# Attention in a fused two-layer kernel: the product of the probabilities with v in two double pieces instead of four single ones

## What is computed

```python
h = gelu(x @ Wi[e] + bi[e]);  x = layernorm(h @ Wo[e] + bo[e] + x) * gamma[e] + beta[e]
x = layernorm(x) * (1 + scale) + shift
q, k, v = x @ Wq + bq, x @ Wk + bk, x @ Wv + bv          # 16 heads of 16 features
scores = q @ k.T / 4 + attention_bias;  scores[masked keys] = -inf
ctx = softmax(scores) @ v                                 # per head: 512 x 512 times 512 x 16
x = x + ctx @ Wo + bo
out = x + gelu2((layernorm(x) * g2 + beta2) @ W1 + b1) @ W2 + b2
```

## Time and profile before

| | us |
|---|---|
| median of 3 runs | 1060.66 (1059.63 to 1061.37) |
| the profiled execution | 1060.56 |
| its span, first to last instruction | 1058.7 |
| attention, 340 to 820 us of the span: PE busy | 464.5 of 480 |
| ACT / DVE / POOL busy in the same stretch | 456.2 / 426.9 / 392.5 |

### The profile page before, as it was taken

The page is one execution under the profiler, slowest core; times in us unless marked ns, Lnnn a source line. Parts: engine busy times, 40 slices in busy tenths (PEclk is TensorE's granted clock), DMA queues, the critical chain, the costliest instruction groups (busy, mean ns, idle before and its releaser), DMA issues.

```text
span 1058.7 us, 19427 instructions
## 1 busy us (share of the span) xinstructions
PE 1006.1 (95%) x6870; PEld 758.3 (72%) x6936; DVE 840.7 (79%) x1966; ACT 790.2 (75%) x1291; POOL 634.2 (60%) x333
## 2 busy tenths in 40 slices
PE   5999999999799999999999999999999799999998
PEld 4789988888565655656666665666666589999997
DVE  6599999998868988989889898998988555555553
ACT  6755577555599899999999999999999344444443
POOL 3565766664246877798787997878877332222110
PEclk9999999999899999999999999999999999999999
DMA  8746788759799999998999989999895131111001
GB/s 234 263 146 222 247 295 301 276 180 378 304 330 398 409 373 358 352 340 322 367 355 340 357 322 362 345 347 343 313 338 199 40 120 60 60 61 40 21 20 40
DMA packets 103249, 269.44 MB, mean 254 GB/s; under 512 B 7522, under 2 KB 63586, under 8 KB 86642
## 3 DMA queue, kind: packets, MB, share of 16 engines
q1 hardware_dynamic: 103154, 268.21, 70.5%
HBM read 217.57 MB, written 50.61 MB: 253 GB/s over the span
## 4 chain that ended last, share of the span: by engine, by line
PE 49%; DVE 12%; DMA 12%; POOL 10%; ACT 8%; issue 7%; SPq 2%; DVEq 0%; ACTq 0%; POOLq 0%
PE psH L540 11%; DMA t_bt<-in_fside_Bx16xSxS 10%; PE psO L540 10%; PE psT L650 9%; POOL t_bt L1423 8%; PE psQ L540 5%; PE psV L663 5%; PE psS L639 4%; ACT t_bt L894 3%; DVE t_x L1026 2%; SPq L255 2%; PE psA L540 2%; ACT t_pt L780 2%; DVE t_bt L1215 2%; PE psX L692 1%
## 5 line engine op out<-in xcount | busy, mean ns | idle before, releaser
L1423 POOL TENSOR_TENSOR t_bt<-t_bt,t_mb 128x1024 f32<-128x1024 f32 x182 | 384.6, 2147 | 89.0 <-DMA t_bt<-in_fside_Bx16xSxS 88.8
L1215 DVE CUSTOM_DVE_ANT_0 t_bt<-psS,t_bt 128x512 f32<-128x512 f32 x512 | 338.2, 684 | 61.1 <-PE psS L639 39.6
L894 ACT ACTIVATE t_bt<-t_bt,t_nm 128x512 f32<-128x512 f32 x512 | 356.6, 732 | 20.4 <-DVE t_nm L1215 20.3
L650 PE MATMUL psT<-t_idf,t_bt 128*128 128x128 f32 x2048 | 308.6, 274 | 5.2 <-issue 2.5
L650 PEld LDWEIGHTS psT<-t_idf,t_bt 128*128 128x128 f32 x2048 | 252.9, 141 | 66.0 <-ACT t_bt L894 12.7
L780 ACT ACTIVATE t_pt<-psT 128x512 f32<-128x512 f32 x317 | 191.2, 603 | 18.9 <-PE psT L650 18.2
L639 PE MATMUL psS<-t_ks,t_qs 128*128 128x512 bf16 x482 | 183.9, 382 | 8.0 <-DVE t_nm L1215 3.7
L1225 DVE COPY t_pt<-psT 128x512 f32<-128x512 f32 x195 | 133.8, 686 | 1.7 <-PE psT L650 1.7
L663 PE MATMUL psV<-t_pt,t_vs 128*17 128x512 f32 x1024 | 134.2, 598 | 0.0
L639 PEld LDWEIGHTS psS<-t_ks,t_qs 128*128 128x128 bf16 x512 | 50.0, 98 | 83.0 <-DVE t_nm L1215 62.8
L1357 POOL TENSOR_SCALAR t_crs<-t_cmv 128x4 f32<-128x4 f32 x8 | 4.2, 519 | 134.8 <-DVE t_cmv L1018 134.8
(11 more groups left out here) (171 smaller groups left out, 2045.1 us busy)
## 6 DMA issues: line engine op xcount, KB each, us to landing
t_bt<-in_fside_Bx16xSxS SPq DMA_DIRECT2D x128, 1024.0 KB, 7.4
sc_qk<-t_parts SPq DMA_DIRECT2D x32, 768.0 KB, 6.6
t_qs<-sc_qk SPq DMA_DIRECT2D x16, 1024.0 KB, 9.8
t_ks<-sc_qk SPq DMA_DIRECT2D x16, 1024.0 KB, 12.2
t_wo_f<-in_L_cond_Wo SPq DMA_DIRECT2D x8, 1024.0 KB, 7.5
sc_qk<-t_parts SPq DMA_DIRECT2D x16, 512.0 KB, 7.4
t_wi_f<-in_L_cond_Wi SPq DMA_DIRECT2D x7, 1024.0 KB, 5.3
sc_v<-t_v SPq DMA_DIRECT2D x8, 544.0 KB, 7.6
```

Of the source, the lines that this page charges most:

```text
L650: ins = e.transpose(psT[turned_bank(n)][:, kk, :], bt[u % NB][:, t, kk * 128:(kk + 1) * 128], idf[:, :])
L894: e.activation(p, p, ACT.Exp, bias=nm[:, n % 16:n % 16 + 1], scale=-1.0).then_inc(a_exp, 1)
L1215: e.tensor_tensor_reduce(bt[u % NB][:, t, :], s, bt[u % NB][:, t, :], -1.0, 3.0e38, ALU.add, ALU.min, nm[:, n % 16:n % 16 + 1]).then_inc(v ...
L1423: e.tensor_tensor(bt[u % NB][:, hs, :], bt[u % NB][:, hs, :], mb[b % 2][:, hs, :], ALU.add).then_inc(g_M, 1)
```

## The change

PSTEP becomes 8, and the block kk is placed by `PSTEP * (kk // 2)`: blocks 0 and 1 run one behind the other at the step where block 0 ran, and blocks 2 and 3 where block 2 ran. All that is placed from the last block uses PSTEP in the place of 3 * PSTEP, and moves four steps forward on its engine.

```diff
-LAG, XLAG, PSTEP, CLAG, SLAG, FIRST = 4, 1, 4, 2, 12, 20
+LAG, XLAG, PSTEP, CLAG, SLAG, FIRST = 4, 1, 8, 2, 12, 20
 # SP: store of the divided product
-                m = n - LAG - CLAG - 2 - 3 * PSTEP - SLAG
+                m = n - LAG - CLAG - 2 - PSTEP - SLAG
 # PE
                 for kk in range(NT):
-                    m = n - LAG - CLAG - PSTEP * kk
+                    m = n - LAG - CLAG - PSTEP * (kk // 2)
                     if 0 <= m < N and m % 16 == 15:
                         context(m // 16, kk)
-                m = n - LAG - CLAG - 2 - 3 * PSTEP
+                m = n - LAG - CLAG - 2 - PSTEP
                 if 0 <= m < N and m % 16 == 15:
                     turn_c_out(m // 16)
 # ACT
-                m = n - LAG - CLAG - PSTEP * (NT - 1)
+                m = n - LAG - CLAG - PSTEP
                 if 0 <= m < N and m % 16 == 15:
                     context_out(m // 16)
 # DVE: context_out; POOL: divide, in the same way
-                m = n - LAG - CLAG - 2 - 3 * PSTEP
+                m = n - LAG - CLAG - 2 - PSTEP
...
-            while at <= N + LAG + CLAG + 3 * PSTEP - 1:
+            while at <= N + LAG + CLAG + PSTEP - 1:
```

## The result

| | us |
|---|---|
| before, median of 5 runs on the same chip | 1060.16 (1058.89 to 1061.37) |
| the changed kernel, median of 5 runs | 1085.10 (1082.52 to 1088.99) |
| ratio, 95% interval | 1.0225 (1.0195 to 1.0256) |
| the profiled execution, the slowest of the five | 1088.99 |
| its span | 1087.2 |

The changed kernel is slower by 25 us. The sign was forecast, the size was not: 1085 lies 18 us above the forecast and 9 above the range.

A forecast was written before the change was run, and what follows sets the result against it. PE was taken to set the pace nearly everywhere, except where a late bias landing holds POOL, DVE and then PE. Terms +14.8 - 11.3 + 3 = +6.5 us on 1060.56 gave 1067 us, range 1057 to 1076.

The forecast's parts named there:

- the divide's place: On POOL, the divide ahead of head 6's mask additions delays tiles 24 and 26: 2.11 us in seven batches, +14.8 us.
- ACT behind a longer block: ACT's stored work just holds through the double block; where it doesn't, PE waits: 3 us in all, bounds 0 and 9.
- what of the savings survives: PE's savings from joints and cv waits, less those lost where a bias landing sets the pace: -11.3 us, bounds -19 and 0.
- tile 24: On DVE, this tile should begin 4.7 us after the first instruction of POOL's divide.
- the room: Between DVE finishing tile 26 and PE beginning tile 29: 0.42 us to spare, taken off the divide's 2.53 us.
- Rival 3: ACT becomes the bound, idling 0.3 us at each of 62 blocks, and PE's savings go too: 1075 us; chance 0.10.
- The joint: On PE, where two blocks meet: each saves 0.22 us, 62 of them 13.6 us of PE's time.
- 20 joints: Joints outside the stretches from q and k load to tile 29, which a bias landing sets: 4.4 us saved.
- The cv waits: At turn_c_out, PE's waits for ACT's copy of a finished product, 5 to 6 us: should be near nothing, 5 us gone.
- PE's wait for DVE and DVE's for POOL: Around the divide: DVE's wait rises from 5 us to about 20; PE stands 2 to 3 us ahead of tiles 27 to 29.
- PE should have stood still: Once in a batch, for 2 to 3 us ahead of tiles 27 to 29, and nowhere else for over 0.5 us.
- PE waiting for exponentials in every group: On PE, behind ACT: named as one of the signs that would show the forecast wrong.

The follow-up runs named there:

- e1: The changed kernel with POOL's divide and SP's store of its product back at their old steps: 1073.34 us, ratio 1.0086.
- e2: The kernel before with only POOL's divide four steps earlier in the seven batches: 1075.81 us, ratio 1.0122.
- e13: e1 with ACT's exponential covering only 256 of the 512 keys (output not the reference's): 1060.79 us, ratio 0.9978.
- e14: The kernel before with ACT's exponential covering only 256 of the 512 keys: 1063.19 us, ratio 0.9987.
- e17: e13 with only one head of eight of q and k loaded again from the third load on: 1045.76 us, ratio 0.9849.
- e18: e14 with only one head of eight of q and k loaded again from the third load on: 1042.99 us, ratio 0.9821.
- e3: e1 with the exponential ahead of the copy of transposes in each of ACT's steps: 1069.47 us, ratio 1.0066.
- e9: e3 with CLAG = 3, all products one tile later: 1065.37 us, ratio 1.0027.
- e10: e9 with four banks for scores and three for transposes instead of three and four: 1065.07 us, ratio 1.0027.

## Why the prediction was right, and where it failed

| term | forecast | measured |
|---|---|---|
| the divide's place | +14.8 | +13.3 (after less e1), +14.1 (e2) |
| ACT behind a longer block | +3 (0 to 9) | about +12 to +14 |
| what of the savings survives | -11.3 (-19 to 0) | about -2.4, not told from 0 (e13 less e14), +2.8 (e17 less e18) |
| sum | +6.5 | +24.9 |

The +14 is e1's 11.6 less the -2.4 of the pair with the short exponential, and 12 if that pair is equal. The measured terms add up to 24.9 because they were taken as differences, so their sum proves nothing. The sign was right thanks to the divide alone: for the double block by itself the forecast had +3 - 11.3 = -8.3 us, and e1 has +11.6.

**The divide** was right in place, cause and size. The order of POOL's program told it, not the diff: 2.53 us forecast and 2.56 found, tile 24 at 4.7 us and 4.94. One reading was off: 521.06 in the earlier trace rows is the start of DVE's last instruction for tile 26, which ends 0.08 later, so the room was 0.34 us and not 0.42, and the term 15.3.

**ACT behind a longer block** is the step that failed, in the sentence "ACT can store up about three tiles of work before PE must wait, some 2.7 us, against a block of 1.96 and 0.65 until new transposes reach it. That just holds." It doesn't. The depth of LAG says how many tiles apart the two engines stand, not what ACT may do while PE is busy with something else. ACT's program is in order, and in it the copy of tile n - 4 stands ahead of the exponential of tile n - 1. From the block's start at 562.73 ACT has 2.12 us of work that it may do, 0.30 left of an exponential, the copy of 0.48 and two exponentials of 1.34, and is through at 564.85. It may go on at 565.43, 2.70 us after the block began: the 0.58 us of idle in that row. The forecast's other side, 1.96 + 0.65 = 2.61, was nearly right; the stored work was not 2.7. How much of the 12 us this stop behind the block makes is less sure than that they are ACT's: e3, which takes it away, brings back 4 us, and e9 8. The rows for it stood in the earlier trace rows: two exponentials between copies, 1.23 us. The other half of the step was to ask who could make it up: ACT had 24 us to spare in 480, and an engine that is busy for 95% recovers from 0.6 us over some twelve tiles of about a microsecond, when the next double block is eight tiles away. Rival 3 was this mechanism, priced at 0.3 us for each of 62 blocks, 1075 in all, and given 0.10. It needed 14 in the place of its 9, and it and the divide add up almost in full: what the rival took off for overlap, 1075 rather than 1081, wasn't there to be taken. Its sum was also loose: 14.8 - 3 + 9 is 20.8 and not 17, and 0.3 us at each of 62 blocks is 18.6 and not 9.

**The joint** was right as a cost and wrong as a saving. The x16 row at 562.73 lasts 1.91 us, and the transposes on its two sides begin 2.60 us apart (562.20, 564.80). Less the 0.65 of a plain tile, a pair adds 1.95 us, against 2 x 1.09 for two lone ones. That is 0.23 saved, as forecast. The Trainium skill's rule (TensorE: Matmul & The Clock Gate, section Part 3: Packing small matmuls), that a load is hidden only if it goes to another group of rows, is not borne out by the x16 rows either; the same section also says that a load for the background weight buffer is pulled ahead of running matmuls, and with that the rows agree. But no pair shows the saving: PE's shorter work became waits, even where ACT was relieved. This is the second step that failed. The forecast let 20 joints count in full because a landing didn't set their stretch. It should have asked what comes second there: exponentials, copies and score banks, each close behind PE, as e3, e9 and e10 showed one after the other.

**Signs named ahead.** The cv waits are gone, as forecast. PE's wait for DVE and DVE's for POOL stand where they should; the latter rose from 7.7 to 15.0 us over 340 to 820 us (17.9 in e2) rather than from 5 to 20. PE should have stood still for over 0.5 us nowhere but ahead of tiles 27 to 29; its waits for exponentials reach 0.7. "PE waiting for exponentials in every group" was named as what would prove the forecast wrong, and it is what the trace shows, near enough (113 waits on the weight loads, 39 on PE, in some 27 groups).

## What to carry to other kernels

Longer blocks on the pacing engine are paid for by its neighbour's queue. Read from the neighbour's own program order what it may do until the block ends (here the rest of an exponential, a copy and two exponentials, 2.1 us against 2.7), and don't take the distance in tiles for it. If the neighbour is nearly as busy as the pace, a stop of half a microsecond comes back as waits a few tiles later (0.56 and 0.50 us behind 0.58 here). And follow every call that is placed from the one you move: here half of the loss was 2.5 us of GpSimd work put between two additions that VectorE was waiting for, and the diff shows the new step of the one and names neither addition.

## What the runs showed of the hardware

- Small matmuls with 17 weight columns, all of 128 rows, run their passes 0.43 us apart within a joined block, with the four loads of the next pass inside the running one (the recorded loads begin at 562.73, 563.17 and 563.60). What a joint saves, 0.23 us, is what beginning and ending one block among other matmuls costs beyond its passes; its parts weren't told apart.
- The DMA share is 0.91 in the attention of the changed kernel (0.93 before); cutting the loads of q and k took it to 0.81 and the time down by 15 us with the double block (e13 to e17) and 20 with single ones (e14 to e18). So this traffic cost 1.4 to 1.9% of the whole in these kernels with the short exponential. The loads left out also stood ahead of a bias in the queue, so the figure isn't a price of the share alone.
- PE can be busy for 477.88 of 480 us with this mixture of matmuls (e18). Against that, the 464.53 of the earlier trace rows leave 13 us in 480. But e18 gained 18 us over the kernel before, more than this idle time, so busy time of PE says only roughly how much room there is.
